# State-space stage of a decoder layer: half of B's products moved to TensorE, more of C's to GpSimd, sums and gate by channels

## The reference

```python
hs   = silu(causal_conv(x @ W_in_states.T, conv_w, 4 taps) + conv_b)   # [b, 1024, l]
gate = x @ W_in_gates.T
dt   = softplus((hs.T @ W_dt.T) @ W_dtproj.T + b_dtproj)
Bm, Cm = hs.T @ W_b.T, hs.T @ W_c.T                                    # [b, l, 16]
dA   = exp(-exp(A_log) * dt)                                           # [b, 1024, l, 16]
dBu  = dt * Bm * hs
h    = scan over l: s = dA * s + dBu
y    = sum over the 16 states of h * Cm, + hs * D
out  = (y * silu(gate)) @ W_out.T
x    = layernorm(x + out)
```

## Time and profile before

| | |
|---|---|
| runs | 3173.22, 3173.97, 3177.13 us; median 3173.97 |
| profiled execution, span from first to last instruction | 3175.0 us |
| granted TensorE clock, mean | 0.977 of full speed |
| busy over the span: PE / DVE / ACT / POOL | 94% / 89% / 76% / 66% |
| the state-space stage | up to about 1748 us of the span |
| DMA engines, mean | 31% busy, 98 GB/s |

### The profile page before, as it was taken

The page is one execution under the profiler, slowest core; times in us unless marked ns, Lnnn a source line. Parts: engine busy times, 40 slices in busy tenths (PEclk is TensorE's granted clock), DMA queues, the critical chain, the costliest instruction groups (busy, mean ns, idle before and its releaser), DMA issues. The chain is left out here.

```text
span 3175.0 us, 47891 instructions
## 1 busy us (share of the span) xinstructions
PE 2991.9 (94%) x16134; PEld 1833.1 (58%) x16134; DVE 2833.2 (89%) x4149; ACT 2419.9 (76%) x4531; POOL 2094.4 (66%) x1207
## 2 busy tenths in 40 slices
PE   7899999999999999999987699999999999799998
PEld 4777677767776777777755244444444444244444
DVE  6999999999999999999998788888888888288887
ACT  4888888888888888888875177777777777577786
POOL 5999999999999999999998234334334334100000
PEclk9999999999999999999998699999999999899999
DMA  4112211222022202220221656655655653221111
GB/s 176 32 46 81 81 49 43 80 81 69 23 80 81 79 13 80 84 81 15 77 96 64 180 163 178 182 181 174 186 181 171 183 180 113 101 77 47 47 41 37
DMA packets 164389, 311.97 MB, mean 98 GB/s; under 512 B 22736, under 2 KB 80208, under 8 KB 164000
## 3 DMA queue, kind: packets, MB, share of 16 engines
q1 hardware_dynamic: 158784, 299.53, 29.6%
q10 hardware_dynamic: 5360, 9.38, 1.0%
HBM read 217.16 MB, written 91.69 MB: 97 GB/s over the span
## 5 line engine op out<-in xcount | busy, mean ns | idle before, releaser
L830 POOL TENSOR_TENSOR bu<-du,bc 128x1024 f32<-128x1024 f32 x512 | 1199.0, 2370 | 32.1 <-DMA bc<-bc_scratch 29.9
L708 ACT ACTIVATE states<-dt,negA 128x256 f32<-128x256 f32 x2048 | 852.8, 463 | 240.2 <-DVE hc L926 229.4
L914 DVE TENSOR_TENSOR_SCAN states<-states,bu 128x512 f32<-128x512 f32 x704 | 821.5, 1212 | 10.5 <-ACT states L708 8.2
L1568 DVE TENSOR_REDUCE mmax<-s_ps 128x1 f32<-128x512 f32 x1024 | 673.0, 686 | 126.1 <-PE s_ps L1288 105.2
L1413 ACT ACTIVATE pt<-s_ps 128x512 f32<-128x512 f32 x1024 | 579.6, 595 | 209.5 <-PE s_ps L1297 203.7
L926 DVE TENSOR_TENSOR hc<-states,bc 128x512 f32<-128x512 f32 x704 | 445.7, 674 | 1.6 <-DMA bc<-bc_scratch 1.6
L1288 PE MATMUL s_ps<-kst,qst 102*128 102x512 bf16 x1024 | 400.5, 393 | 28.6 <-DMA kst<-mask_d 19.3
L526 PEld LDWEIGHTS y_ps<-id_sb,hc 128*128 128x128 f32 x2816 | 330.7, 143 | 122.9 <-DVE hc L926 58.2
L526 PE MATMUL y_ps<-id_sb,hc 128*128 128x128 f32 x2816 | 377.1, 277 | 22.8 <-DVE hc L926 22.8
L1297 PE MATMUL s_ps<-qst,kst 105*128 105x512 bf16 x1024 | 387.4, 382 | 5.8 <-ACT pt L1413 3.9
L839 POOL TENSOR_TENSOR hp<-hp,bc 128x1024 f32<-128x1024 f32 x160 | 379.5, 2372 | 2.8 <-DVE hp L914 1.9
(11 more groups left out here) (172 smaller groups left out, 4170.6 us busy)
## 6 DMA issues: line engine op xcount, KB each, us to landing
bc<-bc_scratch SPq DMA_DIRECT2D x128, 512.0 KB, 5.2
stack_d<-parts SPq DMA_DIRECT2D x180, 256.0 KB, 3.0
qst<-stack_d SPq DMA_DIRECT2D x64, 384.0 KB
kst<-stack_d SPq DMA_DIRECT2D x64, 384.0 KB
x<-xres SPq DMA_DIRECT2D x31, 512.0 KB, 4.8
w_raw<-in_w_ffn SPq DMA_DIRECT2D x48, 256.0 KB, 2.8
w_raw<-in_w_ffn SPq DMA_DIRECT2D x16, 768.0 KB, 7.3
xT_sb<-in_xT SPq DMA_DIRECT2D x16, 512.0 KB, 6.0
```

The lines of the kernel that those rows point to most:

```text
L708: a = act.activation(states[:, bank, first:first + SEQ], dt[:, t, :], ACT.Exp, scale=negA[:, t, c * NS + n:c * NS + n + 1])
L830: pool.tensor_tensor(bu[:, buf, :].rearrange("p (n l) -> p n l", n=NS), du[:, t % (2 * GRP):t % (2 * GRP) + 1, :].to_broadcast([P, NS, SEQ ...
L914: dve.tensor_tensor_scan(dst, src, bu[:, BU_OF[k][0], cols], 0.0, ALU.mult, ALU.add).then_inc(scan_done, 1)
L1568: dve.tensor_reduce(mmax[:, u // HG, c:c + 1], s1_ps[:, n % S_BANKS], AX.X, ALU.max).then_inc(s1_free, 1)
```

## The change

- B: for state groups 1 and 3 (16 steps, PE_B) the product du * B is made on PE. B's 256 values of a state are laid out as two diagonal matrices of 128x128 (`diagB`, 4 KB per partition and group), and du of two tiles is transposed (units "e", in the place of "t") to `duT`; du's transpose times the diagonal gives du * B by channels, straight into PSUM (`weigh_B`, BACK steps ahead, at the end of PE's step). ACT then writes the decay of such a step into SBUF (`decay`, two buffers). The scan takes decay from SBUF and bu from PSUM. POOL keeps the other 16 steps, with two buffers instead of four.
- the diagonals: a zeroed DRAM tensor gets, per batch, two DMAs of 1024 single elements with a step of 2049 elements (`scatter_diagonals`), and two loads of 512 KB (`load_diagonals`). Two of four spreads of B go.
- C: POOL_STEPS has 20 steps instead of 10, so DVE has 12.
- sums, skip term and gate have channels on the partitions: `sum_states` is four plain matmuls of 256 columns with the identity as stationary operand, the gate's projection is 32 plain matmuls of 256 columns, and `finish_y` writes y itself. The sum of a step comes two steps later for all, in `tile_sums`.
- the planner counts the B products and the skip term as fixed costs.

```diff
-PRODUCTS = {"s": HK, "c": TAPS, "g": HK, "l": 2 * DT, "d": GRP, "t": GRP * SEQT, "o": DT}
-COST = {"s": 1, "c": 1, "g": 2, "l": 1, "d": 1, "t": 0.25, "o": 2}
-PER = {"s": DT, "c": DT, "g": 4, "l": 1, "d": GROUPS, "t": GROUPS, "o": SEQT}
+PRODUCTS = {"s": HK, "c": TAPS, "g": GRP * HK, "l": 2 * DT, "d": GRP, "e": GRP * SEQT, "o": DT}
+COST = {"s": 1, "c": 1, "g": 1, "l": 1, "d": 1, "e": 0.5, "o": 2}
+PER = {"s": DT, "c": DT, "g": GROUPS, "l": 1, "d": GROUPS, "e": GROUPS, "o": SEQT}
...
-SHORT = [(0, "d", 1, 0), (3, "t", 3, -1), (6, "d", 2, 0), (11, "t", 0, 0), (12, "d", 3, 0), (18, "t", 1, 0),
-         (23, "d", 0, 1), (26, "t", 2, 0)]
+SHORT = [(0, "d", 1, 0), (5, "e", 1, 0), (6, "d", 2, 0), (11, "e", 2, 0), (12, "d", 3, 0), (17, "e", 3, 0),
+         (23, "d", 0, 1), (28, "e", 0, 1)]
...
-BUS = 4
+BUS = 2
...
-POOL_STEPS = (0, 4, 6, 10, 14, 16, 20, 22, 25, 28)
+POOL_STEPS = tuple(k for k in range(STEPS - 3) if k % 3 != 2)
...
+PE_C = (1, 3)
+POOL_C = tuple(c for c in range(CPT) if c not in PE_C)
+PE_B = [k for k in range(STEPS) if k % CPT in PE_C]
+POOL_B = [k for k in range(STEPS) if k % CPT in POOL_C]
+DECAYS = 2
+B_COST, SKIP_COST = 2 * SEQT, 1
+
+
+def fixed(k):
+
+    return sum(B_COST * ((i + BACK) % STEPS in PE_B) + SKIP_COST * ((i - SUM_AT) % CPT == 0) for i in range(k + 1))
...
+        gate = sb("gate", [P, 2, DT, SEQ])
...
+        bcB = sb("bcB", [P, len(POOL_C), CHUNK])
+        bcC = sb("bcC", [P, CPT, CHUNK])
+        diagB = sb("diagB", [P, len(PE_C), NS, SEQT, P])
+        duT = sb("duT", [P, 2, GRP * SEQT, P])
+        decay = sb("decay", [P, DECAYS, CHUNK])
...
+            def scatter_diagonals(f):
+
+                rows = diag_d.rearrange("(p x) -> p x", x=len(PE_C) * CHUNK + 1)
+                for i, c in enumerate(PE_C):
+                    if f > 0:
+                        sp.wait_ge(diag_in[c], f * 16)
+                    src = bc_scratch[2 * c * NS:(2 * c + 1) * NS, :].rearrange("n l -> (n l)").rearrange("(x p) -> p x", p=P)
+                    sp.dma_start(rows[:, i * CHUNK:(i + 1) * CHUNK:P], src, allow_slow_non_contiguous=True).then_inc(diag_out, 16)
+
+            def load_diagonals(f, c):
+                i = PE_C.index(c)
+                if f > 0:
+                    sp.wait_ge(bu_turned, HALVES * pe_inputs(f - 1, STEPS - CPT + c))
+                sp.wait_ge(diag_out, (f + 1) * len(PE_C) * 16)
+                rows = diag_d[0:P * len(PE_C) * CHUNK].rearrange("(p x) -> p x", p=P)
+                sp.dma_start(diagB[:, i].rearrange("p n t l -> p (n t l)"), rows[:, i * CHUNK:(i + 1) * CHUNK])\
+                  .then_inc(diag_in[c], 16)
...
             save_bc(0)
+            scatter_diagonals(0)
             for c in range(CPT):
-                spread(c, 0, b_in)
-                spread(c, 1, c_in)
+                if c in POOL_C:
+                    spread_B(c)
+                spread_C(c)
+            for c in PE_C:
+                load_diagonals(0, c)
...
+                    scatter_diagonals(f)
                 if active(f):
-                    for c in range(CPT):
-                        sp.wait_ge(bu_done, (b + 1) * STEPS - CPT + c + 1)
-                        spread(c, 0, b_in)
+                    for c in POOL_C:
+                        sp.wait_ge(bu_done, pool_inputs(b, STEPS - CPT + c))
+                        spread_B(c)
+                    for c in PE_C:
+                        load_diagonals(f, c)
...
                     elif kind == "g":
-                        m = pe.matmul(proj[:, :], xT_sb[:, k, i % 2 * P:(i % 2 + 1) * P],
-                                      win_sb[:, k, 1, i // 2 * HID:(i // 2 + 1) * HID], start=start, stop=stop)
+                        t, h = GRP * i + k // HK, k % HK
+                        m = pe.matmul(proj[:, k // HK * SEQ:(k // HK + 1) * SEQ], win_sb[:, h, 1, t * P:(t + 1) * P],
...
-                    elif kind == "t":
-                        m = pe.transpose(proj[:, k * P:(k + 1) * P], yT[:, k // SEQT, k % SEQT, :], id_sb[:, :])
+                    elif kind == "e":
+                        m = pe.transpose(proj[:, k * P:(k + 1) * P],
+                                         du[:, i % 2 * GRP + k // SEQT, k % SEQT * P:(k % SEQT + 1) * P], id_sb[:, :])
...
                     pe.wait_ge(y_ready, b * DT + t)
-                for i in range(SEQT):
-                    pe.matmul(y_ps[:, i, :], u[:, par, t, i * P:(i + 1) * P], diagD[:, t, :],
-                              start=(i == 0), stop=False, skip_group_check=True)
+                pe.matmul(y_ps[:, :], diagD[:, t, :], u[:, par, t, :], start=True, stop=False, skip_group_check=True)
...
-                    for i in range(SEQT):
-                        m = pe.matmul(y_ps[:, i, :], src[:, n * SEQ + i * P:n * SEQ + (i + 1) * P], id_sb[:, :],
-                                      start=False, stop=(c == CPT - 1 and n == NS - 1), is_transpose=True,
-                                      skip_group_check=True)
+                    m = pe.matmul(y_ps[:, :], id_sb[:, :], src[:, n * SEQ:(n + 1) * SEQ],
+                                  start=False, stop=(c == CPT - 1 and n == NS - 1), skip_group_check=True)
...
+            def tile_sums(b, par, k):
+
+                if k % CPT == 0:
+                    skip_term(b, par, k // CPT)
+                sum_states(b, k)
+
+            def weigh_B(b, k):
+
+                t, c = k // CPT, k % CPT
+                if c == PE_C[0] and t % GRP == 0:
+                    pe.wait_ge(ev["e"], seq("e", b, t // GRP))
+                if t == 0:
+                    pe.wait_ge(diag_in[c], (b + 1) * 16)
+                before = bank_before(b, k)
+                for half in range(HALVES):
+                    if before is not None and before[1] in POOL_STEPS:
+                        pe.wait_ge(scan_done, half_of(*before, half))
+                    elif before is not None:
+                        pe.wait_ge(hc_dve, half_product(*before, half))
+                    dst = states[:, bank_of_half(k, half), :].rearrange("p (n l) -> p n l", l=SEQ)
+                    rows = slice(half * NS // HALVES, (half + 1) * NS // HALVES)
+                    for i in range(SEQT):
+                        m = pe.matmul(dst[:, :, i * P:(i + 1) * P], duT[:, t // GRP % 2, t % GRP * SEQT + i, :],
+                                      diagB[:, PE_C.index(c), rows, i, :], start=(i == 0), stop=(i == SEQT - 1))
+                    m.then_inc(bu_turned, 1)
...
                         unit(pos % PROJ, kind, i, 0, 0, 0, PRODUCTS[kind])
                 pe.wait_ge(set_up, 2)
                 pe.wait_ge(wout_in, 16)
+                for k in range(BACK):
+                    if k in PE_B:
+                        weigh_B(0, k)
...
-                    if k % CPT == 0:
-                        skip_term(b, par, k // CPT)
-                    if k not in POOL_STEPS:
-                        sum_states(b, k)
-                    if k % CPT and k - SUM_AT in POOL_STEPS:
-                        sum_states(b, k - SUM_AT)
+                    if k >= SUM_AT:
+                        tile_sums(b, par, k - SUM_AT)
+                    elif b > 0:
+                        tile_sums(b - 1, 1 - par, k - SUM_AT + STEPS)
+                    ahead, step = (b, k + BACK) if k + BACK < STEPS else (b + 1, k + BACK - STEPS)
+                    if active(ahead) and step in PE_B:
+                        weigh_B(ahead, step)
 
             def tail():
+                for k in range(STEPS - SUM_AT, STEPS):
...
+                elif kind == "e":
+                    last = f * STEPS + GRP * CPT * (i - 1) - 1
+                    if last > 0:
+                        act.wait_ge(bu_turned, HALVES * pe_inputs(last // STEPS, last % STEPS))
+                    act.activation(duT[:, i % 2].rearrange("p a l -> p (a l)"), proj[:, :], ACT.Copy).then_inc(ev["e"], 1)
...
-                b0, k0 = (b, k - BACK) if k >= BACK else (b - 1, k - BACK + STEPS)
...
-                    if not (isinstance(b, int) and b == 0 and k < BACK):
-                        if k0 in POOL_STEPS:
-                            act.wait_ge(scan_done, half_of(b0, k0, half))
+                    if before is not None and (k in PE_B or before[1] in POOL_STEPS):
+                        act.wait_ge(scan_done, half_of(*before, half))
+                    elif before is not None:
+                        act.wait_ge(hc_dve, half_product(*before, half))
+                    for i in range(NS // HALVES):
+                        n = half * NS // HALVES + i
+                        if k in PE_B:
+                            dst = decay[:, PE_B.index(k) % DECAYS, n * SEQ:(n + 1) * SEQ]
                         else:
-                            act.wait_ge(hc_dve, half_product(b0, k0, half))
-                    for i in range(NS // HALVES):
-                        n, bank, first = half * NS // HALVES + i, bank_of_half(k, half), i * SEQ
```

(50 more changed lines are left out.)

97 lines of the change are left out of this document (54 added, 43 removed).

## The result

| | before | after |
|---|---|---|
| median of 4 runs each, us | 3175.38 (3173.22 to 3177.13) | 3959.72 (3958.77 to 3963.36) |
| profiled span, us | 3175.0 | 3958.8 |
| period of the state-space stage, us per batch | 104.2 | 156.7 |

The ratio is 1.2475, 95% interval 1.2457 to 1.2492: slower by 784 us. The forecast was 3959. One of the twelve runs of the third kernel of experiment 7 took 6831.86 us, for a reason that stayed unknown, and is in none of its numbers.

The account below looks back on a forecast made before the run. PE was taken to become the bound: 153.9 us of work plus 2.8 idle gave a 156.7 us period; with front +5 and last batch +12, the span rose 785 to 3960, so 3959 us, range 3894 to 4075.

Parts of the forecast that it names:

- The sums: PE's sums over the states: eight plain instructions a step instead of eight transposes, +27.2 us a batch.
- The products with B: PE's new products with B in 16 steps, eight instructions of 1.73 us in all each: +27.7 us a batch.
- The idle time: PE's waits in a steady batch: 2.8 us taken, bounds 0 and 8.
- Item (1): At step 0 PE's dt unit waits for DVE's residad add to free its bank: about 2.2 us.
- (2): B's product for step k+2 waits for DVE's scan k: fits, with 0.5 us to spare at step 7.
- (3): PE's skip term of the next tile waits for gating: about 3.1 us, against 3.4 or more of other work.
- (4): The low-rank unit starts a step before ACT has applied Silu to u: 0 to 1 us.
- Rival A: Handoffs: PE stands about 1 us at each of 16 B products, or diagonals land late; 4200 us, chance 0.09.
- Front, first and last batch: Stage's ends: front +5 us (+1 to +15), first batch 140.2 us, last batch 133 us, +12 (0 to +25).
- POOL and DVE would allow 90: Work left on POOL and on DVE after the change: 90 us a batch each, below PE's 153.9.
- rival C: Faster: PE has over 55 us free a batch, POOL and DVE set some 92.5 us; 3004 us, chance 0.03.

Follow-up runs that it names:

- third kernel of experiment 7: After with float32r sums and B products, each step's sum issued ahead of the units except where a tile begins: 3175.27 us.
- experiment 4: Sums moved ahead of the units: in after 3932.03 us; in after with B on PE for one group and a third POOL buffer 3738.25 us.
- experiment 1: The kernel before with only its f32 transposes in the sums turned into plain products with the identity: 3547.56 us.
- experiment 6: After with the sums' operands as float32r: 3392.28 us; then the products with B in float32r too: 3256.20 us.
- experiment 5: After with ten of C's products on POOL instead of twenty: 3967.61 us.
- last kernel of experiment 6: After with the operands of both the sums and the products with B as float32r: 3256.20 us.
- the four of experiment 7: After with float32r sums and B products, plus: two of four states summed 3201.19; sums first 3144.15; sums first but at tiles 3175.27; that with two states 3135.27 us.
- third and fourth of 7: After with float32r sums and B products, sums first but at tiles: 3175.27 us; the same with two of four states summed: 3135.27 us.
- experiment 2: After with B's products on PE for state group 1 alone, 8 of 32 instead of 16: 3865.7 us.

## Why the prediction was right

**PE's work.** The step that carried the forecast was the count in the earlier trace rows: a plain f32 matmul is two instructions, a transpose one. It gave 153.9 us a batch and 154.6 were measured with PE never idle (experiment 4). Its two large terms held. The sums: in experiment 1 they add 28.2 us by the count (sixteen instructions of 128 columns; +27.2 for the eight of 256 in after), and the period grew by 24.5, with PE's former spare time (5.2 us) absorbing the rest. The products with B, +27.7: 1.73 us each from start to start, 26.2 by the difference of two kernels (experiment 4).

**The idle time** was 2.1 us for 2.8. Item (1), the residual add, is the whole of it within half a microsecond: 17.9 us in 11 times, 1.6 each. Items (2), the products with B, and (3), the gating, came out at nothing, as worked out; (4) was not seen either. Rival A's mechanism is real but needs PE to be fast: in experiment 6, with a step 1 to 2 us shorter, PE waits 36 times in 800 us at B's products for a scan. In after the scan is done by the time it is asked for. That the period came out as 156.7 to the tenth is luck: the work was 0.7 us more than counted and the idle time 0.7 less.

**POOL, DVE and C.** Both were forecast near 58% and show 57.4 and 58.5. Moving C's ten products costs or gives nothing that matters (experiment 5), as taken.

**Front, first and last batch.** The body begins at 63.97 (65 forecast), the first diagonal's product at 59.62 (61), the last batch at 2397.0 (2399) and takes 134.5 (133). These small misses cancel, and part of the front's hit is luck, for its path was another. I had read nine transfers in a row out of the earlier trace rows, 2 us each, with xT the last. In fact the start of xT's transfer waits for PE's last gate product, in before (7.8 us of SP's time) and in after, one row of SP's waits up to 70 us:
```profile
SPq L388 <- PE proj L557: 6.7, 1, 6.7
```
PE didn't wait for xT in after. The body's start follows from the first diagonal at 59.62, B's product behind it (to 62.49) and a dt unit (to 63.97), at a granted clock of 0.60 from 59.6 to 63.9 us, after 2.13 us of waiting.

**DMA.** I had bounded the scatters' landing between 1.5 and 12 us and taken 5. The page lists them, and its counts of packets under 512 B are 56032 for 22736:
```profile
diag_d<-bc_scratch SPq DMA_DIRECT2D x32, 4.0 KB, 4.3
diagB<-diag_d SPq DMA_DIRECT2D x32, 512.0 KB, 3.8
```
That is 33296 more packets, close to the 32 x 1024 = 32768 elements: one packet for each element, which fits the one descriptor for each element that the Trainium skill states (DMA: Bandwidth & Descriptors, Rules for kernel authors). But one lands in 4.3 us, and the two of the front are both down 5.7 us after the first was issued, near the 5 taken and far from the bound of 12 for two. Past the front PE never waits for a diagonal.

**What was wrong** stands in a rival. "POOL and DVE would allow 90", and with it rival C's 3004, added up work and gave nothing for the handoffs in two-deep rings. The last kernel of experiment 6 and the four of experiment 7 held PE's work at 94 us, or 87 with half the sums, and got periods of 102 to 110, never below 101.7. The lowest time was 3135, where rival C had 3004. What the rival would have given with PE all but free is not shown, for PE is busy for 91% even there. It didn't touch the forecast, since PE needed 154.6; in a case where PE gets cheaper it would have been the term that fails. The second kernel of experiment 6 and the third and fourth of 7 missed with this term, and experiment 2 with a two-deep ring too, POOL's.

What stays open: which part of the 102 us is the hp ring, which the product order on POOL and which the half clock that follows PE's waits.

## What to carry to other kernels

Count the instructions that the profile shows for a matmul, not those in the code, and price them from start to start in a stretch without idle time; a plain f32 product is two, a transpose one, so a sum turned from transposes into plain products doubled here. An engine that shows 97% busy beside two that show 98% must be costed before it is given work that relieves the other two. Where engines hand two buffers back and forth, the sum of an engine's work isn't the period it can hold: issue first what gives a buffer back.

## What was not expected of the hardware

A float32r matmul of 256 columns is one instruction and takes 0.117 us, against 0.432 for the two of plain f32: little more than the 0.108 that I had set for one end, far from the 0.216 of the other. The 0.163 in the expectations of experiment 7 came from 0.65 us for a group of four, which holds the end of the plain instruction before it (experiment 6), and so PE's work stands 8 us too high there (102 for 94).

In the second kernel of experiment 6 PE's granted clock fell to half for 3 to 7 us in every batch, at the end of a wait of 2.3 us for the residual add. In experiment 7's kernel with the sums first that wait is 1.3 us, and the clock stayed at 1.00 in all its steady batches. A change of the order within a step gave back some clock beside the wait itself.

ACT's Exp of 128x256 is 29 ns slower into SBUF than into PSUM, hidden here; groups of ACT in after, 400 to 1600 us:
```profile
L809 ACT ACTIVATE states<-dt,negA 128x256 f32<-128x256 f32 x492 | 211.2, 466 | 441.9 <-DVE hp L1019 274.6 <-DVE hc L1032 167.2
L809 ACT ACTIVATE decay<-dt,negA 128x256 f32<-128x256 f32 x489 | 207.2, 495 | 0.4
```
The forecast had taken both as equal, 463 and 460 ns, from the earlier trace rows.
